# Two graph layers on one core: no memsets between groups of gathers, and a first layer with paired slot products and stationary type weights

## The chip, the cores and the metric

The kernel runs on one core of a Trainium2 chip. The metric is the device time of one execution in microseconds. Before the change the median of three runs is 4864.73 us (4861.53 to 4864.73).

## The reference, cut to what matters

There are 12,500 nodes with 64 features, and 212,500 edges sorted by destination, each with 8 attributes and one of 16 types. All is fp32.

```python
h = jnp.maximum(_layernorm(x, axis=-1), 0.0)
for r in range(16):                                    # first layer
    mask = etypes == r
    msg = msg + h[src] * mask[:, None] @ weight[r]     # weight: 16 x 64 x 64
x = x + segment_sum(msg, dst)
h = jnp.maximum(_layernorm(x, axis=-1), 0.0)
msg_input = concatenate([h[src], h[dst], edge_attr], axis=1)   # second layer
msg = relu(msg_input @ W1 + b1) @ W2 + b2
x = x + segment_sum(msg, dst)
```

## The kernel before, in words

Edges are handled in groups of 1024: 8 tiles (`T`) of 128 edges (`P`), 208 groups (`G`) in all. Loops run over 26 turns (`NIT`) of 8 groups (`U`); the first turn of each layer is written out, the others run in a hardware loop, the last one of POOL and PE again by itself. Each engine has its own program; semaphores order them.

**Gathers.** For each tile POOL issues one indirect DMA (`gather`, L710) that fetches 128 rows of 64 fp32 from a table in DRAM (`h_table` in the first layer, `p_table` in the second) into `rows[:, u, t]`, so 8 for a group. `rows` has 8 buffers, one for each `u`. At the end of each group in `turn_of_rows` and `turn_of_groups` POOL writes zeros into a tile that nobody reads, `spacer` (L743, L763), and before the next group it waits until that write is done (`spaced`). It then waits for `slots_summed`, so that group k is gathered only when group k-3 has been summed by PE (first layer), or for `pre_added`, so that it is gathered only when DVE has added the rows of group k-3 (second layer). The gathers of groups 8 to 15 stand before `turn_of_rows`: they have no spacer, and wait only until the group 8 places earlier is summed. `wait_apart` is a wait followed by an increment of a semaphore that nobody reads.

**First layer.** DVE makes `onehot` (L1095): for each edge a row of 256 zeros with a one at type*16 + offset of its destination within 16 nodes. In `sum_slots` (L1379) PE multiplies, for each tile, the rows (stationary, 128x64) by the onehot (moving, 128x256). Even tiles go to partitions 0 to 63 of the result, odd ones to 64 to 127, and odd and even groups have PSUM banks of their own (two each, `slot_ps`). ACT copies each half of a group into `slots` (L890). In `apply_types` (L1386), for each pair of groups, PE adds up 16 products, one for each type: `slots` of this type is stationary (128x128), the type's weights, twice on the diagonal of a 128x128 block, move. ACT copies the result to `nodes_t` (L894), and PE puts it into windows of 128 nodes with two products of 256 columns (`place_nodes`, L1393), with a matrix `place` that DVE makes from `key_p` (L1161). DVE adds the windows to `acc` (`add_windows`, L1158).

The order on PE within `step` is: `sum_slots` of group u; then, at even u, `apply_types` of the pair before, at odd u `place_nodes` of the pair before. At u = 4 and u = 7 of each turn PE also does the parts of a chunk of 480 nodes that are then complete (L1329, L1336, L1344, L1346). ACT's order is: both halves of group u, then at even u the copy for `place_nodes`.

**Second layer.** For each group PE does `products` (L1461, L1462), `place_z` (L1470), `sum_group` (L1466) and `pick_q` (L1456); DVE adds the gathered rows (L1219), masks and reduces (L1226, L1230), adds a window (L1239), and spreads q (L1243); ACT does the relu (L951).

Of the kernel before, what the change touches and what calls it, by code (L numbers as in the profile page):

```python
# [6 lines left out]
def gnn_kernel(nc, x, src, dst, edge_attr, edge_type, rel_weight, w1, b1, w2, b2, out):  # L7
# [39 lines left out]
    T2 = T // 2  # L47
    Q = 2 * T2
# [14 lines left out]
    NWL = 2 + 4 + T + 4  # L63
# [10 lines left out]
    with ctx:  # L74
# [26 lines left out]
        heads_i = sb("heads_i", [Q, NP, 2], i32)  # L101
        heads_f = sb("heads_f", [Q, NP, 2], fp32)
        key_p = sb("key_p", [P, NP, 2], fp32)
        place = sb("place", [P, 2, 2 * W1], fp32)
        nodes_t = sb("nodes_t", [P, 2 * D], fp32)
        spread = sb("spread", [Q, P], fp32)
        spread_first = sb("spread_first", [Q, P], fp32)
        slot_row_i = sb("slot_row_i", [1, P], i32)
        slot_row = sb("slot_row", [1, P], fp32)
        idx = sb("idx", [P, U, T], i32)  # L110
        spacer = sb("spacer", [P, T * D], fp32)
        rows = sb("rows", [P, U, T, D], fp32)
        onehot = sb("onehot", [P, 2, T, C0], fp32)
        slots = sb("slots", [P, 2, R, P], fp32)
# [27 lines left out]
        w_types = sb("w_types", [P, R, 2 * D], fp32)  # L142
# [55 lines left out]
        key_ps = ps[:, 7, 0:2 * NP]  # L198
# [58 lines left out]
        spaced = sem("spaced")  # L257
# [4 lines left out]
        heads_in = sem("heads_in")  # L262
        heads_float = sem("heads_float")
        key_turned = sem("key_turned")
        key_copied = sem("key_copied")
        typed = sem("typed")
        nodes_copied = sem("nodes_copied")
        place_made = sem("place_made")
        placed = sem("placed")
# [189 lines left out]
        def scattered_products(pe, n):  # L459
            def tile(t):  # L460
                pe.wait_ge(sc["dst_float", n], t + 1)
                pe.matmul(ps[:, 0, 0:P], s_dstf.broadcast_to([P, P]), ident[:], start=True, stop=True)
                if n == 0:
# [3 lines left out]
                    for half in range(2):  # L467
                        r = slice(half * R // 2, (half + 1) * R // 2)
                        last = pe.matmul(ps[:, 2 + half, :].rearrange("p (r m) -> p r m", m=D), s_gt[0:D, :], w_types[0:D, r, 0:D], start=True, stop=True)
# [68 lines left out]
        def _(sp):  # L538
# [23 lines left out]
            of_pairs = dst[0:(NP - 1) * 2 * GE].rearrange("(m q h e) -> q m h e", q=Q, h=2, e=P)[:, :, :, 0]  # L562
            for h in range(2):
                sp.dma_start(heads_i[:, 0:NP - 1, h], of_pairs[:, :, h], allow_slow_non_contiguous=True).then_inc(heads_in, 16)
            for b, first in ((0, (G - 2) * GE), (1, LAST)):
                sp.dma_start(heads_i[b * T2:(b + 1) * T2, NP - 1, :], dst[first:first + GE].rearrange("(q h e) -> q h e", h=2, e=P)[:, :, 0],
                             allow_slow_non_contiguous=True).then_inc(heads_in, 16)
# [112 lines left out]
        def _(pool):  # L680
            for v in (ident[:], again[:], spread[:], spread_first[:]):
                pool.memset(v, 0.0).then_inc(pool_chain, 1)
            pool.memset(blocks[:], 1.0).then_inc(pool_chain, 1)
            pool.wait_ge(pool_chain, 5)
# [6 lines left out]
            pool.wait_ge(pool_chain, 6)  # L691
# [7 lines left out]
            by_head = lambda v: v.rearrange("q (h w) -> q h w", w=W0)  # L699
            pool.affine_select(out=by_head(spread[:]), in_=by_head(spread[:]), compare_op=ALU.not_equal, fill=1.0, base=0,  # L700
                               pattern=[[-1, Q], [0, W0]], channel_multiplier=1).then_inc(consts_made, 1)
            by_first = lambda v: v.rearrange("q (h w) -> q h w", h=2)
            pool.affine_select(out=by_first(spread_first[:]), in_=by_first(spread_first[:]), compare_op=ALU.not_equal, fill=-1.0, base=0,
                               pattern=[[-T2, 2], [0, P // 2]], channel_multiplier=1).then_inc(consts_made, 1)
            pool.iota(by_first(slot_row_i[:]), pattern=[[P, 2], [1, P // 2]], base=0, channel_multiplier=0).then_inc(consts_made, 1)
            pool.wait_ge(consts_made, 10)
# [16 lines left out]
            with pool.If(fits > 0):  # L723
# [8 lines left out]
                pool.sem_inc(spaced, 1)  # L732

                def turn_of_rows(it, last=False):
                    for u in range(U):
                        wait_apart(pool, spaced, (it - 2) * U + u + 1)
# [6 lines left out]
                        pool.memset(spacer[:], 0.0).then_inc(spaced, 1)  # L743
# [8 lines left out]
            with pool.If(fits > 0):  # L752
                def turn_of_groups(it, last=False):
                    for u in range(U):
                        wait_apart(pool, spaced, (NIT - 2 + it) * U + u + 1)
# [7 lines left out]
                        pool.memset(spacer[:], 0.0).then_inc(spaced, 1)  # L763
# [11 lines left out]
        def _(act):  # L775
            act.sem_inc(relu_made, AHEAD)
            act.sem_inc(pq_copied, 1)

            act.wait_ge(blocks_cleared, 2)
            loads = [(w_types[h * D:(h + 1) * D, :, h * D:(h + 1) * D], rel_weight.rearrange("r k m -> k r m")) for h in range(2)]  # L780
# [99 lines left out]
            with act.If(fits > 0):  # L880
                def group(it, u):
# [16 lines left out]
                for u in range(U):  # L898
                    group(0, u)
                    if u % 2 == 0 and u >= 2:  # L900
                        copy_nodes(u // 2 - 1)
# [637 lines left out]
```

## Time and profile before

| what | value |
|---|---|
| median of three runs | 4864.73 us |
| profiled execution | 4855.4 us |
| its span, first to last instruction | 4853.2 us |
| POOL busy | 3380.0 us (70%) |
| PE busy | 2787.7 us (57%) |
| PE weight loads busy | 1549.3 us (32%) |
| DVE busy | 1468.1 us (30%) |
| ACT busy | 577.2 us (12%) |
| granted TensorE clock, mean | 0.692 of 2.4 GHz |

The profiled execution lies 9.3 us under the median of the runs, and 2.2 us of it are outside its span. The engines work side by side, so their busy times don't add up to the span. POOL's issuing of DMAs counts as busy (as DMA_INDIRECT); the transfers themselves do not.

### The profile page before, as it was taken

How to read it: one execution, taken by the hardware profiler on the slowest of the kernel's cores; microseconds unless marked ns; L12 is line 12 of the kernel's file. 1: busy time of each engine (PE TensorE's matmuls, PEld its weight loads, DVE VectorE, ACT ScalarE, POOL GpSimd, SP SyncE). 2: the span in 40 equal slices, each digit the busy share in tenths (PEclk: the TensorE clock that was granted, in tenths of full speed). 3: DMA queues.
4: the chain of work that ended last, by engine and by line, in shares of the span. 5: the costliest groups of instructions: out<-in, count | busy, mean ns of one | idle time of the engine just before them, and what ended most of it. 6: DMA issues, size and time to landing. Idle time of an engine off the chain costs nothing.

```text
span 4853.2 us, 37713 instructions
## 1 busy us (share of the span) xinstructions
PE 2787.7 (57%) x10310; PEld 1549.3 (32%) x10310; DVE 1468.1 (30%) x2002; ACT 577.2 (12%) x1139; POOL 3380.0 (70%) x3742
## 2 busy tenths in 40 slices
PE   2565665656556655656565565565555655656555
PEld 1343343434334433434332232222222222222222
DVE  6322222222222222222232333233332332332333
ACT  3111111111111111111110010010000000100000
POOL 7567667666666666676757767777777777777776
PEclk9777776677767777776766666666666666666666
DMA  4111111111111111111111112111111111211111
GB/s 102 20 27 25 25 27 25 25 27 25 25 25 27 25 26 26 25 25 27 25 29 31 29 31 31 29 31 31 29 31 29 32 31 29 32 31 32 29 31 28
DMA packets 391187, 144.15 MB, mean 30 GB/s; under 512 B 321650, under 2 KB 337323, under 8 KB 391163
## 3 DMA queue, kind: packets, MB, share of 16 engines
q0 software_dynamic: 106304, 109.07, 11.8%
q1 hardware_dynamic: 282245, 34.18, 4.9%
q10 hardware_dynamic: 2614, 0.62, 0.1%
q8 instruction: 10, 0.16, 0.0%
q14 instruction: 14, 0.11, 0.0%
HBM read 129.03 MB, written 12.83 MB: 29 GB/s over the span
## 4 chain that ended last, share of the span: by engine, by line
POOL 39%; issue 26%; another core or an unknown queue 17%; PE 12%; DVE 3%; ACT 1%; SPq 1%; DMA 1%; POOLq 0%; DVEq 0%; ACTq 0%
POOL rows L710 36%; PE ps L1379 4%; PE ps L1386 2%; POOL spacer L763 2%; PE ps L1462 1%; PE ps L1461 1%; PE ps L1393 1%; POOL spacer L743 1%; PE ps L1344 1%; PE ps L1346 1%; DVE z_slot L1230 0%; PE ps L1466 0%; DVE q_blk L1243 0%; DVE slots L1219 0%
## 5 line engine op out<-in xcount | busy, mean ns | idle before, releaser
L710 POOL DMA_INDIRECT rows<-p_table,idx x1661 | 1579.6, 951 | 702.0 <-issue 631.3
L710 POOL DMA_INDIRECT rows<-h_table,idx x1533 | 1452.1, 947 | 693.8 <-issue 506.6
L1461 PE MATMUL ps<-w_attr,attr_t 64*128 64x512 f32 x416 | 400.9, 1063 | 1004.8 <-DVE q_blk L1243 694.7
L1379 PE MATMUL ps<-onehot,rows 128*64 128x256 f32 x3328 | 661.8, 512 | 101.2 <-DMA rows<-h_table,idx 50.8
L1386 PE MATMUL ps<-w_types,slots 128*128 128x128 f32 x3328 | 518.2, 307 | 226.5 <-issue 201.6
L1095 DVE TENSOR_TENSOR onehot<-key,ps 128x2048 f32<-128x2048 f32 x209 | 474.6, 2279 | 439.5 <-remote 389.5
L1386 PEld LDWEIGHTS ps<-w_types,slots 128*128 128x128 f32 x3328 | 462.3, 215 | 314.1 <-issue 282.5
L1219 DVE TENSOR_TENSOR slots<-ps,rows 128x512 f32<-128x512 f32 x208 | 143.9, 692 | 1378.1 <-DMA rows<-p_table,idx 831.5
L1379 PEld LDWEIGHTS ps<-onehot,rows 128*64 128x64 f32 x3328 | 333.6, 179 | 349.4 <-issue 287.8
L1461 PEld LDWEIGHTS ps<-w_attr,attr_t 64*128 64x128 f32 x416 | 96.8, 288 | 1041.8 <-issue 1041.4
L1462 PE MATMUL ps<-q_blk,onehot 128*128 128x512 f32 x416 | 422.2, 1118 | 0.0
L890 ACT COPY slots<-ps 128x512 f32<-128x512 f32 x416 | 239.3, 588 | 1057.9 <-remote 766.6
L1466 PE MATMUL ps<-relus,onehot 128*128 128x512 f32 x416 | 339.8, 913 | 0.9 <-DVE z_blk L1226 0.9
L1158 DVE TENSOR_TENSOR acc<-acc,ps 64x128 f32 x208 | 58.2, 280 | 918.1 <-remote 645.7
L951 ACT ACTIVATE relus<-slots 128x512 f32<-128x512 f32 x208 | 131.1, 630 | 1663.2 <-DVE slots L1219 1511.3
L1393 PE MATMUL ps<-place,nodes_t 128*64 128x256 f32 x416 | 158.6, 521 | 277.8 <-ACT nodes_t L894 142.1
L1230 DVE TENSOR_REDUCE z_slot<-z_blk 128x64 f32<-128x512 f32 x208 | 209.1, 1005 | 0.1
L1226 DVE TENSOR_TENSOR z_blk<-ps,blocks 128x512 f32<-128x512 f32 x208 | 142.8, 687 | 193.5 <-remote 136.7
L1462 PEld LDWEIGHTS ps<-q_blk,onehot 128*128 128x128 f32 x416 | 100.8, 301 | 295.6 <-issue 295.6
L1393 PEld LDWEIGHTS ps<-place,nodes_t 128*64 128x64 f32 x416 | 70.4, 184 | 354.2 <-issue 185.7
L1470 PEld LDWEIGHTS ps<-onehot,z_slot 128*65 128x65 f32 x416 | 95.5, 230 | 231.5 <-issue 229.0
L1456 PEld LDWEIGHTS ps<-q_win,onehot 128*128 128x128 f32 x416 | 110.8, 267 | 176.4 <-issue 176.4
(142 smaller groups left out, 1971.8 us busy)
## 6 DMA issues: line engine op xcount, KB each, us to landing
rows<-p_table,idx POOLq DMA_INDIRECT x1661
rows<-h_table,idx POOLq DMA_INDIRECT x1533
attr<-in_edge_attr_dram SPq DMA_DIRECT2D x52, 128.0 KB
q_win<-q_table SPq DMA_DIRECT2D x208, 32.0 KB
p_table<-pq_out SPq DMA_DIRECT2D x25, 120.0 KB
q_table<-pq_out SPq DMA_DIRECT2D x25, 120.0 KB
out_dram<-xs SPq DMA_DIRECT2D x25, 120.0 KB
xs<-in_x_dram SPq DMA_DIRECT2D x6, 480.0 KB, 6.4
```

Source lines behind the costliest of these rows:

```text
L710: pool.indirect_dma_start(rows[:, u, t, :], None, table, bass.IndirectOffsetOnAxis(ap=at, axis=0)).then_inc(s, 16)
L890: act.copy(to, slot_ps[:, u % 2, t, :].rearrange("p t (r w) -> p t r w", w=W0)).then_inc(slots_copied, 1)
L1095: dve.tensor_tensor(onehot[:, b], key0[:, bass.ds(g, 1), :].rearrange("p a (t c) -> p (a t) c", c=1).broadcast_to([P, T, C0]), iota_ps.rea ...
L1219: dve.tensor_tensor(presum[:, u % 2, 0:T * D], pre_ps[:, u % 2, :], rows[:, u].rearrange("p t d -> p (t d)"), ALU.add).then_inc(pre_added, 1)
L1226: dve.tensor_tensor(by_tile(z_blk[:]), by_tile(z_ps), own_tile, ALU.mult).then_inc(z_masked, 1)
L1230: dve.tensor_reduce(z_slot[:, u, 0:D], z_blk[:].rearrange("p (t d) -> p d t", d=D), X, ALU.add).then_inc(z_slotted, 1)
L1379: last = pe.matmul(slot_ps[t % 2 * D:(t % 2 + 1) * D, b, t // 2, :], rows[:, u, t, :], onehot[:, b, t, :], start=True, stop=True)
L1386: last = pe.matmul(nodes_ps, slots[:, b, r, :], w_types[:, r, :], start=(r == 0), stop=(r == R - 1))
L1393: last = pe.matmul(win_ps, nodes_t[:, h * D:(h + 1) * D], place[:, h, :], start=(h == 0), stop=(h == 1))
L1461: pe.matmul(pre_ps[:, u % 2, :], attr_t[half, u // 2, :], w_attr[half].rearrange("k j d -> k (j d)"), start=True, stop=False)
L1462: pe.matmul(pre_ps[:, u % 2, :], oh1_t[:, u, :], q_blk[:, u % 2, :], start=False, stop=True).then_inc(pre_made, 1)
L1466: pe.matmul(z_ps, oh1[:, u, :], relu_rows[:, u % 2, :], start=True, stop=True).then_inc(z_made, 1)
```

## The change

The memsets of `spacer` and the waits for them go, in both layers. In the first layer:

- `sum_slots` multiplies two tiles at a time: the rows of both are stationary (128x128), the onehots of both move (128x512). The result holds four blocks, of which two are wanted (tile 2j's rows with its own onehot, and 2j+1's with its own). There are 4 products a group, each fills a bank, and all groups use the same 4 banks. So PE waits, before the first half of a group, until ACT has copied the first half of the group before, and likewise with the second half.
- ACT takes the wanted blocks out, with 4 copies of 64 partitions and 256 elements for each half in place of one of 128 partitions and 512.
- `apply_types` has the weights of two types as the stationary operand (128x64) and moves `slots` of the pair of groups (256 columns), 8 products a pair. Its result is 64x256, features by slots, so it must be turned: ACT copies it (`copy_sums`), PE turns it (`turn_nodes`, two transposes, ahead of `sum_slots` at odd u), ACT copies it again (`copy_nodes`, now ahead of the group at odd u), and `place_nodes` places it, with two products of 128 columns.
- `place` is made from `key_w`, which was there already, with half the columns. The loads, products and copies that made `key_p` go, and the clearing of `w_types`.

```diff
-        slot_ps = ps_all[:, 0:4 * 512].rearrange("p (b t c) -> p b t c", b=2, t=T2)
-        nodes_ps = ps[:, 4, 0:2 * D]
+        slot_ps = ps_all[:, 0:4 * 512].rearrange("p (j c) -> p j c", j=TH)
+        sums_ps = ps[0:D, 4, 0:2 * P]
+        nodes_ps = ps[:, 4, 2 * P:2 * P + 2 * D].rearrange("p (b m) -> p b m", m=D)
...
 def turn_of_rows(it, last=False):
     for u in range(U):
-        wait_apart(pool, spaced, (it - 2) * U + u + 1)
         if u % B == 0:
             wait_apart(pool, batch_in[u // B], 16 * (it - 1))
         wait_apart(pool, slots_summed, 2 * AHEAD + 2 * (it * U + u - 2))
         for t in range(SKIP if last and u == U - 1 else 0, T):
             gather(h_table, u, t, rows_in[u])
-        pool.memset(spacer[:], 0.0).then_inc(spaced, 1)
...
 def turn_of_groups(it, last=False):
-        wait_apart(pool, spaced, (NIT - 2 + it) * U + u + 1)
...
         for j in range(SKIP if last and u == U - 1 else 0, T):
             gather(p_table, u, j, rows_in[u])
-        pool.memset(spacer[:], 0.0).then_inc(spaced, 1)
...
     for half in range(2):
         act.wait_ge(slots_summed, 2 * AHEAD + 2 * g + half + 1)
-        t = slice(half * T2 // 2, (half + 1) * T2 // 2)
-        to = slots[:, u // 2 % 2].rearrange("p r (b t w) -> p b t r w", b=2, t=T2)[:, u % 2, t]
-        act.copy(to, slot_ps[:, u % 2, t, :].rearrange("p t (r w) -> p t r w", w=W0)).then_inc(slots_copied, 1)
+        j = slice(half * TH // 2, (half + 1) * TH // 2)
+        to = slots[:, u // 2 % 2].rearrange("p r (b j a w) -> p b a j r w", b=2, a=2, w=W0)[:, u % 2]
+        for a in range(2):
+            of = slot_ps[a * D:(a + 1) * D, j, a * C0:(a + 1) * C0].rearrange("p j (r h w) -> p h j r w", h=2, w=W0)
+            for h in range(2):
+                last = act.copy(to[h * D:(h + 1) * D, a, j], of[:, h])
+        last.then_inc(slots_copied, 1)
+
+def copy_sums(m):
+    act.wait_ge(typed, AHEAD + m + 1)
+    act.copy(sums_t[:], sums_ps).then_inc(sums_copied, 1)

 def copy_nodes(m):
-    act.wait_ge(typed, AHEAD + m + 1)
+    act.wait_ge(nodes_turned, m + 1)
     act.copy(nodes_t[:], nodes_ps).then_inc(nodes_copied, 1)
...
     for u in range(U):
+        if u % 2 == 1:
+            copy_nodes(it * (U // 2) + u // 2 - 1)
         group(it, u)
         if u % 2 == 0:
-            copy_nodes(it * (U // 2) + u // 2 - 1)
+            copy_sums(it * (U // 2) + u // 2 - 1)
...
 def sum_slots(g, it, u, first):
-    if u % 2 == 0 and (not first or u >= 2):
-        wait_apart(pe, slots_copied, 2 * (g - 1))
+    wait_apart(pe, slots_copied, 2 * g + 1)
     pe.wait_ge(onehot0, g + 1)
     pe.wait_ge(rows_in[u], ...)
-    for t in range(T):
-        last = pe.matmul(slot_ps[t % 2 * D:(t % 2 + 1) * D, b, t // 2, :], rows[:, u, t, :], onehot[:, b, t, :], start=True, stop=True)
-        if t % 4 == 3:
+    for j in range(TH):
+        if j == TH // 2:
+            wait_apart(pe, slots_copied, 2 * g + 2)
+        last = pe.matmul(slot_ps[:, j, :], rows[:, u, 2 * j:2 * j + 2, :].rearrange("p t d -> p (t d)"),
+                         onehot[:, b, 2 * j:2 * j + 2, :].rearrange("p t c -> p (t c)"), start=True, stop=True)
+        if j % 2 == 1:
             last.then_inc(slots_summed, 1)

 def apply_types(m, b):
-    pe.wait_ge(slots_copied, 4 * (m + 1))
-    for r in range(R):
-        last = pe.matmul(nodes_ps, slots[:, b, r, :], w_types[:, r, :], start=(r == 0), stop=(r == R - 1))
+    pe.wait_ge(slots_copied, 4 * m + 6)
+    for r in range(R2):
+        last = pe.matmul(sums_ps, w_pairs[:, r, :], slots[:, b, r, :], start=(r == 0), stop=(r == R2 - 1))
     last.then_inc(typed, 1)
+
+def turn_nodes(m):
+    wait_apart(pe, sums_copied, m + 1)
+    for b in range(2):
+        last = pe.transpose(nodes_ps[:, b, :], sums_t[:, b * P:(b + 1) * P], ident[0:D, 0:D])
+    last.then_inc(nodes_turned, 1)

 def place_nodes(m):
-    for h in range(2):
-        last = pe.matmul(win_ps, nodes_t[:, h * D:(h + 1) * D], place[:, h, :], start=(h == 0), stop=(h == 1))
+    for b in range(2):
+        last = pe.matmul(win_ps[:, b * W1:(b + 1) * W1], nodes_t[:, b, :], place[:, b, :], start=True, stop=True)

 def step(it, u, first=False):
+    if u % 2 == 1 and (not first or u >= 2):
+        turn_nodes(m - 1)
     sum_slots(k, it, u, first)
```

## Rows read from the trace of the kernel before

**Rows 1.** The page: span, and busy times with shares.

```profile
span 4853.2 us, 37713 instructions
PE 2787.7 (57%) x10310; PEld 1549.3 (32%) x10310; DVE 1468.1 (30%) x2002; ACT 577.2 (12%) x1139; POOL 3380.0 (70%) x3742
```

**Rows 2.** Groups by line: busy us, mean ns of one, idle time before and releasers.

```profile
L710 POOL DMA_INDIRECT rows<-p_table,idx x1661 | 1579.6, 951 | 702.0 <-issue 631.3 <-POOL spacer L763 63.5 <-DVE slots L1219 7.3
L710 POOL DMA_INDIRECT rows<-h_table,idx x1533 | 1452.1, 947 | 693.8 <-issue 506.6 <-remote 101.7 <-POOL spacer L743 59.3
```

**Rows 3.** Timeline of POOL across a spacer: start, length, what, idle before.

```profile
226.47 0.95 POOL L710 DMA_INDIRECT rows<-h_table,idx  x1 [0.96 <-issue]
...
235.23 0.95 POOL L710 DMA_INDIRECT rows<-h_table,idx  x1 [0.30 <-issue]
236.17 0.55 POOL L743 MEMSET spacer<- 128x512 f32 x1
237.69 0.95 POOL L710 DMA_INDIRECT rows<-h_table,idx  x1 [0.97 <-issue]
```

**Rows 4.** Gathers alone by stretch: length, busy us (count), granted clock, DMA share, GB/s.

```profile
1300.00:2300.00 1000.00, 650.54 (x687) 0.71 0.13 26
2500.00:3500.00 1000.00, 665.84 (x702) 0.66 0.19 30
```

**Rows 5.** Timeline of POOL where groups 8 to 15 are gathered without spacers.

```profile
138.41 0.95 POOL L710 DMA_INDIRECT rows<-h_table,src_tab  x1 [4.54 <-remote]
...
157.16 0.95 POOL L710 DMA_INDIRECT rows<-h_table,src_tab  x1 [0.30 <-issue]
161.39 0.95 POOL L710 DMA_INDIRECT rows<-h_table,src_tab  x1 [3.28 <-remote]
```

**Rows 6.** Timeline of PE and ACT in that stretch.

```profile
143.02 3.84 PE L1386 MATMUL ps<-w_types,slots 128*128 128x128 f32 x32
146.78 2.15 PE L1379 MATMUL ps<-onehot,rows 128*64 128x256 f32 x16
160.97 0.27 ACT L894 COPY nodes_t<-ps 128x128 f32<-128x128 f32 x1 [17.24 <-remote]
161.29 1.54 PE L1393 MATMUL ps<-place,nodes_t 128*64 128x256 f32 x3 [12.36 <-ACT nodes_t L894]
```

**Rows 7.** Waits, longest first: engine, line, releaser: us in total, times, longest.

```profile
ACT nodes_t L894 <- remote: 735.2, 79, 27.6
```

**Rows 8.** Timeline of PE while POOL stood still.

```profile
202.65 1.95 PE L1379 MATMUL ps<-onehot,rows 128*64 128x256 f32 x16
204.43 0.81 PE L1393 MATMUL ps<-place,nodes_t 128*64 128x256 f32 x3
...
207.11 3.84 PE L1386 MATMUL ps<-w_types,slots 128*128 128x128 f32 x32
```

**Rows 9.** By stretch: length, busy us (count) of PE, PEld, DVE, ACT, POOL, granted clock.

```profile
194.00:214.00 20.00, 18.84 (x154) 14.46 (x150) 12.14 (x13) 6.20 (x13) 0.02 (x1) 1.00 0.02 3
```

**Rows 10.** Timeline of PE at the lower clock, in the first layer and in the second.

```profile
1542.55 3.68 PE L1379 MATMUL ps<-onehot,rows 128*64 128x256 f32 x16
1546.16 3.66 PE L1386 MATMUL ps<-w_types,slots 128*128 128x128 f32 x19
...
3023.03 2.07 PE L1462 MATMUL ps<-q_blk,onehot 128*128 128x512 f32 x2
```

**Rows 11.** Groups by line: ACT's copies and a chunk's products, first layer.

```profile
L890 ACT COPY slots<-ps 128x512 f32<-128x512 f32 x416 | 239.3, 588 | 1057.9 <-remote 766.6 <-PE ps L1379 240.6 <-issue 50.6
...
L1344 PE MATMUL ps<-w1ab,h_t 128*120 128x256 f32 (+1 forms) x104 | 61.3, 695 | 173.8 <-issue 90.5 <-ACT h_t L860 83.3
...
L860 ACT COPY h_t<-ps 128x240 f32<-128x240 f32 (+1 forms) x26 | 9.5, 365 | 43.4 <-remote 37.3 <-issue 4.4 <-PE ps L1336 1.7
```

**Rows 12.** Second layer: DVE's addition of the gathered rows (by line), PE's products (in time).

```profile
L1219 DVE TENSOR_TENSOR slots<-ps,rows 128x512 f32<-128x512 f32 x208 | 143.9, 692 | 1378.1 <-DMA rows<-p_table,idx 831.5 <-remote 275.2 <-PE ps L1462 170.7
...
3031.84 2.04 PE L1461 MATMUL ps<-w_attr,attr_t 64*128 64x512 f32 x2 [4.68 <-DVE q_blk L1243]
```

More of the change, by code:

```diff
@@ L62, in gnn_kernel @@
     EG = 6
-    NWL = 2 + 4 + T + 4
+    NWL = 3 + 4 + T + 4
     GB = G + B
@@ L100, in gnn_kernel @@
         base_row = sb("base_row", [1, G], i32)
[L101 to L109, printed above, removed]
+        place = sb("place", [P, 2, W1], fp32)
+        sums_t = sb("sums_t", [D, 2 * P], fp32)
+        nodes_t = sb("nodes_t", [P, 2, D], fp32)
         idx = sb("idx", [P, U, T], i32)
-        spacer = sb("spacer", [P, T * D], fp32)
         rows = sb("rows", [P, U, T, D], fp32)
         onehot = sb("onehot", [P, 2, T, C0], fp32)
-        slots = sb("slots", [P, 2, R, P], fp32)
+        slots = sb("slots", [P, 2, R2, 2 * P], fp32)
         relus = sb("relus", [P, 2, T, KA], fp32)
@@ L141, in gnn_kernel @@
         zrows = sb("zrows", [P, D], fp32)
-        w_types = sb("w_types", [P, R, 2 * D], fp32)
+        w_types = sb("w_types", [D, R, D], fp32)
+        w_pairs = sb("w_pairs", [P, R2, D], fp32)
         w_attr = sb("w_attr", [2 * T * F, T, D], fp32)
@@ L468, in tile @@
                         r = slice(half * R // 2, (half + 1) * R // 2)
-                        last = pe.matmul(ps[:, 2 + half, :].rearrange("p (r m) -> p r m", m=D), s_gt[0:D, :], w_types[0:D, r, 0:D], start=True, stop=True)
+                        last = pe.matmul(ps[:, 2 + half, :].rearrange("p (r m) -> p r m", m=D), s_gt[0:D, :], w_types[:, r, :], start=True, stop=True)
                 else:
@@ L698, in _ @@
             pool.iota(limit_i[:], pattern=[[HG, 2]], base=-DONE, channel_multiplier=1).then_inc(consts_made, 1)
[L699 to L706, printed above, removed]
+            pool.wait_ge(consts_made, 7)
             def gather(table, u, t, s, of=None):
@@ L776, in _ @@
             act.sem_inc(relu_made, AHEAD)
+            act.sem_inc(slots_copied, 2)
             act.sem_inc(pq_copied, 1)
-            act.wait_ge(blocks_cleared, 2)
-            loads = [(w_types[h * D:(h + 1) * D, :, h * D:(h + 1) * D], rel_weight.rearrange("r k m -> k r m")) for h in range(2)]
+            act.wait_ge(blocks_cleared, 1)
+            loads = [(w_pairs[h * D:(h + 1) * D, :, :], rel_weight.rearrange("(r h) k m -> h k r m", h=2)[h]) for h in range(2)]
+            loads += [(w_types[:], rel_weight.rearrange("r k m -> k r m"))]
             loads += [(w1ab[half * D:(half + 1) * D, half, a * D:(a + 1) * D], w1[a * D:(a + 1) * D, :])
@@ L920, in _ @@
                 turn_of_groups(NIT - 1, last=True)
+                copy_sums(NP - 1)
+                copy_ht(NC - 1, chunk_nodes)
                 copy_nodes(NP - 1)
-                copy_ht(NC - 1, chunk_nodes)
                 act.wait_ge(layer0_summed, 1)
@@ L1004, in _ @@
             dve.tensor_copy(idx[:, 0:EG, :].rearrange("p u t -> p (u t)"), ps[:, 5, 0:EG * T]).then_inc(first_idx, 1)
-            dve.memset(w_types[:], 0.0).then_inc(blocks_cleared, 1)
             def check_edges():
@@ L1160, in make_place @@
                 def make_place(m):
-                    dve.tensor_tensor(place[:], key_p[:, bass.ds(m, 1), :].rearrange("p a (h c) -> p (a h) c", c=1).broadcast_to([P, 2, 2 * W1]),
-                                      iota_ps.rearrange("p (a c) -> p a c", a=1).broadcast_to([P, 2, 2 * W1]), ALU.is_equal).then_inc(place_made, 1)
+                    dve.tensor_tensor(place[:], key_w[:, bass.ds(2 * m, 2)].rearrange("p (b c) -> p b c", c=1).broadcast_to([P, 2, W1]),
+                                      iota_ps[:, 0:W1].rearrange("p (a c) -> p a c", a=1).broadcast_to([P, 2, W1]), ALU.is_equal).then_inc(place_made, 1)
                 def step(it, u, first=False):
@@ L1421, in _ @@
                 turn_h(NC - 1, chunk_nodes)
+                turn_nodes(NP - 1)
                 place_nodes(NP - 1)
```

43 lines of the change are left out of this document (12 added, 31 removed).

## The prediction, made before the changed kernel was run

> **What bounds the kernel now.** I read the page first. POOL is the busiest engine, 3380.0 us of 4853.2, PE follows with 2787.7 [rows 1]. The groups by line say that POOL's time is gathers: 3322 of them, of which the 1661 of the second layer take 951 ns each and the 1533 of the first layer's main part 947, and that the idle time ahead of them is mostly "issue", which waits for nothing [rows 2]. The timeline shows the beat. Gathers follow each other after 0.95 + 0.30 = 1.25 us. At a group's end stands a memset of 0.55 us, and 0.97 us pass before the next gather; from 226.47 to 237.69 is 11.22 us for a group [rows 3]. By stretch, the first layer makes 687 gathers in 1000 us, 8 x 1000/687 = 11.64 us a group, the second 702, so 11.40 us [rows 4]. So in both layers POOL runs near its own beat of 11.22; the other engines add 0.42 and 0.18 us a group. The page's 57% for PE is a mean over two layers with different work: what matters is whether PE and its partners keep up at a shorter beat.
>
> **The change, part by part.**
>
> *Spacers.* A group would then be 8 x 1.25 = 10.0 us, if its waits cost nothing on POOL. The 16 gathers from 138.41 are such a stretch: the last starts at 157.16, 18.75 us later, which is 15 x 1.25, with a group's boundary between them at no cost [rows 5]. So the beat falls by 1.22 us a group. 192 groups of the first layer (those after 8 to 15) and 208 of the second have a spacer: 400 x 1.22 = 488 us is the most that can be won. From below, nothing: what ends the wait may be the others.
>
> *Slot products, PE.* Before, 16 instructions (each fp32 product is recorded as two) of 256 columns take 1.95 us at the full clock, 2.4 GHz [rows 8, 9], and 3.68 us at 1.2 GHz [rows 10]. That is 0.12 us for each. After, 8 instructions of 512 columns with 128 weights. The row nearest to them is L1462, two of 512 columns in 2.07 us at the lower clock; L1393 had three of 256 columns in 0.81 us at the full one, an instruction each 0.21 to 0.27. So I take 0.43 us at the full and 0.9 at the lower clock for each: 3.4 and 7.2 us a group. This part adds 1.5 us to a group at one clock and 3.5 at the other. The reason is in these rows: before, instructions of 256 columns into different halves of the partitions advance by 0.12 us, those of L1393 into the same half by at least 0.21. The Trainium skill, "TensorE: Matmul & The Clock Gate", section "Part 3: Packing small matmuls — row/col tiling", says that products with few weight columns, put into different column groups of the array, run side by side. It speaks against this change, which gives that up and computes two unwanted blocks of four; by it alone the slot products would cost twice what they did, as the rows say too.
>
> *Types, PE.* Before, 32 instructions of 128 columns with 128 weights took 3.84 us [rows 8], at the lower clock 3.66 x 32/19 = 6.2. After, 16 of 256 columns with 64 weights: 3.4 at the full clock (0.21 each) and 6.8 at the lower. No gain to speak of in columns; half the weight loads.
>
> *Placing and turning, PE.* Two products of 128 columns for two of 256 save 0.4 to 0.85 us a pair, the two transposes cost 0.3 to 0.5: nothing.
>
> So a pair of groups costs PE 6.8 + 3.4 + 0.8 = 11 us at the full clock, 14.4 + 6.8 + 1.4 = 22.6 at the lower, where before it was 8.6 and 15. The parts for node chunks come on top: L1344 has 61.3 us in 104 pairs, 0.6 us [rows 11], the bias products next to it the like, the turns less, so I estimate 1.5 us a pair. The new beat of POOL is 20.0 us a pair. It fits at the full clock and doesn't at the lower one. The first layer had 0.71 on average [rows 4]; at 0.71 the pair takes 11 / 0.71 = 15.5 us, and 17.0 with the chunks, which fits with 3.0 us left.
>
> *ACT.* For each half 4 copies of 256 elements in place of one of 512 (588 ns); the nearest is L860 with 365 ns for 240 elements [rows 11]. 8 x 0.38 = 3.0 us a group for 1.2. A pair has 0.4 + 0.3 us of copies more (L894 takes 0.27 [rows 6]). 6.8 us of 20: hidden, but the copy of a half, 1.5 us, now stands between PE's groups, because the banks are shared. PE has the other half to do meanwhile, 1.7 us at least, so that wait is near zero as long as ACT hears of the end of a half at once.
>
> *Waits.* New is that PE waits at each odd u, ahead of the slot products, for ACT's `copy_sums`, which waits for the end of `apply_types`. Behind that wait stand the group's products, then ACT's copies, then POOL's gathers of three groups on. At least it costs 0.4 us of copy and some 0.1 of signals, a pair. At most it costs what ACT waits for that end today: 735.2 us in 79 times, 9.3 each [rows 7], since PE's instructions are recorded well before others may start on them. I take 2 us a pair, near the low end, because there are half the weight loads in the stretch behind which these delays stand, and because the second layer, with few and long products, shows little of them.
>
> *Before the loops* the clearing of `w_types` and the making of `key_p` go: a few us. I take 4.
>
> *The sum.* First layer: 17.0 + 2 = 19.0 us of PE a pair against 20.0 of POOL, so they catch each other at times. I take 11.0 us a group, 1.0 over the beat for 0.42 today: 192 x (11.64 - 11.0) = 123 us. Second layer: only the beat changes. DVE waits for the DMA of rows 831.5 us in 208 groups, 4.0 each, though only a part of this can be given up [rows 12]: PE's products (2.04 + 2.07) and DVE's addition stand in a ring with it. I take 10.5, 0.5 over the beat: 208 x (11.40 - 10.5) = 187 us. With the 4, 314 us: the profiled execution goes from 4855.4 to 4541, and the median of the runs from 4864.7 to **4551 us**. For both layers together: each 0.1 us a group is 40 us.
>
> **The rivals.**
>
> *POOL's beat alone decides.* The others add what they add today: 10.42 and 10.18 us a group, 4864.7 - 488 - 4 = 4373. For it: DVE and ACT are far from full [rows 1]. Against it: PE's 19.0 of 20.0. Chance 0.2 for all below 4460.
>
> *The gap was needed.* In the stretch without spacers PE's products of types end by the record at 146.86, yet ACT starts on them at 160.97, when POOL had come to rest after 157.16; POOL then goes on at 161.39, 22.98 us after 138.41, so 11.49 us a group, no shorter than with spacers [rows 5, 6]. When POOL issues without a pause, PE's results may be reported late until POOL must stop. For both layers: 192 x 0.15 less and 208 x 0.09 more, 4850 us. For it is that it is the one place where the trace shows what the change makes. Against: it has another set of waits (8 groups ahead), first passes through written-out code, and PE has the old products. Chance 0.2 for 4700 to 4875.
>
> *PE's ring becomes the bound in the first layer; slower.* It needs the pair's PE time with its waits to go over 23.3 us. Its work is 17.0, so the first layer gets slower when the waits take 6.3 us a pair. With the 9.3 that ACT waits today it is 26.3 us a pair, 13.15 a group: 192 x 1.51 = 290 us more. Against 187 + 4 won elsewhere that makes 4964 us, and 5151 if the second layer gains nothing. The kernel as a whole gets slower at 8.3 us of waits (191/192 = 0.99 a group over 11.64). Against it: a PE that works more is granted the higher clock more often (full in the 20 us when it was busy for 18.84 [rows 9]), and POOL at rest lets its results through. Chance 0.25 for all above 4875.
>
> **How the numbers follow.** The forecast, 4460 to 4700, has 0.35, the three rivals 0.2, 0.2 and 0.25. A difference of 0.2% (10 us) is about what a measurement of this kernel can tell. Faster by more: the forecast, the first rival, and 0.12 of the second: 0.66. Within: 0.04. Slower: 0.05 of the second and the third, 0.30. The range for 8 in 10 leaves out 0.04 below 4370 and 0.15 above 4990, and it is wide because the cases have both signs; the forecast's own is 4460 to 4700.
>
> **What would show it.** Right: POOL has no idle time but 0.30 between most gathers; 10.4 to 10.6 us a group in the second layer and some 11 in the first; slot products 8 instructions in 3.4 to 7 us; DVE's wait for DMA in the second layer shrinks by about 0.9 us a group; clock in the first layer above 0.71. Wrong: idle times of 3 us and more ahead of the first gather of each second group, ended by PE or DVE; `copy_sums` starting 5 us or more after the end of L1386; PE waiting at `turn_nodes`, with the clock still at 0.7.

## The result, and the profile after

The changed kernel takes 5270.03 us (median of four runs, 5226.03 to 5293.56) against 4864.39 for the kernel before: 1.0825 of it, 95% interval 1.0751 to 1.0899. It is slower by 406 us; the forecast of 4551 and its range are missed, on the wrong side.

The page of the changed kernel: its span, the busy times, and the granted clock in 40 slices.

```profile
span 5278.6 us, 32488 instructions
...
PE 2864.8 (54%) x7184; PEld 1316.7 (25%) x7184; DVE 1454.3 (28%) x1998; ACT 991.8 (19%) x2490; POOL 3152.3 (60%) x3337
...
PEclk9877787787877877877856666666666666666666
```

POOL is busy for 228 us less, most of it the memsets, and PE for only 77 us more than in [rows 1]; yet the span is 425 us longer. Only ACT is nearer to its limit than before (19% for 12%), and it is far from it. The groups by line of the same page:

```profile
L688 POOL DMA_INDIRECT rows<-p_table,idx x1661 | 1572.5, 947 | 1050.1 <-DVE slots L1199 527.9
L688 POOL DMA_INDIRECT rows<-h_table,idx x1533 | 1447.2, 944 | 985.6 <-issue 462.5
...
L1356 PE MATMUL ps<-onehot,rows 128*128 128x512 f32 x1664 | 972.2, 735 | 125.1 <-ACT slots L867 76.9
L867 ACT COPY slots<-ps 64x256 f32<-64x256 f32 x1664 | 608.9, 366 | 1061.0 <-remote 599.9
...
L1370 PE MATMUL ps<-ident,sums_t 64*128 64x64 f32 x208 | 39.7, 283 | 825.4 <-ACT sums_t L872 695.7
...
L1364 PE MATMUL ps<-slots,w_pairs 128*64 128x256 f32 x1664 | 390.6, 389 | 1.0 <-ACT slots L867 1.0
```

The gathers last as long as in [rows 2]. POOL's idle time ahead of them has grown by 640 us, and the memsets that are gone gave back 217 of it. Second layer: 1572.5 + 1050.1 = 2622.6 us, before 1579.6 + 702.0 = 2281.6 and 208 memsets of 0.55, 2396. That is 227 us more. First layer: 2432.8 against 2145.9 + 192 x 0.55 = 2251.5, 181 more. Together that is 408 of the 425. So more of the loss lies in the second layer, in which only the memsets and their waits changed. By stretch, as in [rows 4]:

```profile
1300.00:2300.00 1000.00, 606.01 (x643) 0.79 0.12 24
...
2700.00:4700.00 2000.00, 1215.89 (x1286) 0.64 0.17 28
```

8 x 1000/643 = 12.44 us for a group of the first layer (11.64 before), and 8 x 2000/1286 = 12.44 in the second too (11.41 before, 1402 gathers in the same stretch). The stretch of the second layer starts at 2700 here, because the first layer's gathers now go on until some 2610. The new waits of the trace (engine, line, releaser: us in total, times, longest):

```profile
PE ps L1448 <- DVE q_blk L1223: 1026.9, 125, 21.0
PE ps L1370 <- ACT sums_t L872: 695.7, 54, 18.9
ACT slots L867 <- remote: 599.9, 84, 16.3
POOL rows L688 <- DVE slots L1199: 527.9, 80, 11.4
POOL rows L688 <- PE ps L1356: 342.2, 32, 39.0
```

In the second layer PE now waits 1026.9 us for DVE (694.7 before), and POOL 527.9 us (7.3 in [rows 2]). What such a wait looks like in the first layer, from the timeline (start, length, what, idle time before):

```profile
1484.23 3.67 PE L1364 MATMUL ps<-slots,w_pairs 128*64 128x256 f32 x16
...
1500.22 0.94 POOL L688 DMA_INDIRECT rows<-h_table,idx  x1 [0.30 <-issue]
1505.26 0.36 ACT L872 COPY sums_t<-ps 64x256 f32<-64x256 f32 x1 [13.27 <-remote]
1505.77 0.45 PE L1370 MATMUL ps<-ident,sums_t 64*128 64x64 f32 x2 [17.88 <-ACT sums_t L872]
...
1513.68 0.94 POOL L688 DMA_INDIRECT rows<-h_table,idx  x1 [12.52 <-PE ps L1356]
```

The products by types end at 1487.90. ACT, which waits for nothing else, starts on them at 1505.26, 17.4 us later and 4.1 us after POOL's last gather ended. Then everything follows at once. It is the picture of [rows 5, 6], in the loop now, and POOL stands for 12.52 us in place of 3.28.

### The profile page after: what moved, and what is told of

Its sections match the earlier page's. It is cut to its first block, busy times and chain, and to the rows that moved or that the text cites. A ratio compares the mean times of both kernels' runs of the same rounds, so it can differ in the third digit from the quotient of the medians.

```text
span 5278.6 us, 32488 instructions
## 1 busy us (share of the span) xinstructions
PE 2864.8 (54%) x7184; PEld 1316.7 (25%) x7184; DVE 1454.3 (28%) x1998; ACT 991.8 (19%) x2490; POOL 3152.3 (60%) x3337
## 3 DMA queue, kind: packets, MB, share of 16 engines
q0 software_dynamic: 106304, 109.07, 10.8%
## 4 chain that ended last, share of the span: by engine, by line
another core or an unknown queue 34%; PE 32%; issue 19%; DVE 8%; ACT 5%; DVEq 1%; ACTq 0%; DMA 0%; SPq 0%
PE ps L1356 14%; PE ps L1449 5%; PE ps L1448 4%; ACT slots L867 4%; PE ps L1364 3%; PE ps L1453 3%; DVE z_slot L1210 2%; DVE q_blk L1223 2%; DVE slots L1199 1%; DVEq L1214 1%; PE ps L1457 1%; PE ps L1377 1%; PE ps L1370 1%; DVE onehot L1182 1%
## 5 line engine op out<-in xcount | busy, mean ns | idle before, releaser
L688 POOL DMA_INDIRECT rows<-p_table,idx x1661 | 1572.5, 947 | 1050.1 <-DVE slots L1199 527.9
L1448 PE MATMUL ps<-w_attr,attr_t 64*128 64x512 f32 x416 | 362.0, 966 | 1266.5 <-DVE q_blk L1223 1026.9
L1356 PE MATMUL ps<-onehot,rows 128*128 128x512 f32 x1664 | 972.2, 735 | 125.1 <-ACT slots L867 76.9
L867 ACT COPY slots<-ps 64x256 f32<-64x256 f32 x1664 | 608.9, 366 | 1061.0 <-remote 599.9
L1356 PEld LDWEIGHTS ps<-onehot,rows 128*128 128x128 f32 x1664 | 368.8, 235 | 583.0 <-issue 578.2
L1370 PE MATMUL ps<-ident,sums_t 64*128 64x64 f32 x208 | 39.7, 283 | 825.4 <-ACT sums_t L872 695.7
L1364 PE MATMUL ps<-slots,w_pairs 128*64 128x256 f32 x1664 | 390.6, 389 | 1.0 <-ACT slots L867 1.0
L1364 PEld LDWEIGHTS ps<-slots,w_pairs 128*64 128x64 f32 x1664 | 223.7, 140 | 212.7 <-issue 70.1
L1370 PEld LDWEIGHTS ps<-ident,sums_t 64*128 64x128 f32 x208 | 26.5, 177 | 858.7 <-issue 858.7
L1223 DVE TENSOR_TENSOR q_blk<-ps,blocks 128x512 f32<-128x512 f32 x208 | 142.1, 683 | 217.8 <-remote 193.3
L928 ACT COPY attr_t<-ps 128x128 f32<-128x128 f32 x105 | 27.8, 264 | 748.9 <-remote 624.6
```

The costliest lines, as they stand in the source:

```text
L688: pool.indirect_dma_start(rows[:, u, t, :], None, table, bass.IndirectOffsetOnAxis(ap=at, axis=0)).then_inc(s, 16)
L867: last = act.copy(to[h * D:(h + 1) * D, a, j], of[:, h])
L1223: dve.tensor_tensor(by_tile(q_blk[:, u % 2, :]), q_ps.rearrange("p (a d) -> p a d", a=1).broadcast_to([P, T, D]), own_tile, ALU.mult).then ...
L1356: last = pe.matmul(slot_ps[:, j, :], rows[:, u, 2 * j:2 * j + 2, :].rearrange("p t d -> p (t d)"), onehot[:, b, 2 * j:2 * j + 2, :].rearra ...
L1364: last = pe.matmul(sums_ps, w_pairs[:, r, :], slots[:, b, r, :], start=(r == 0), stop=(r == R2 - 1))
L1448: pe.matmul(pre_ps[:, u % 2, :], attr_t[half, u // 2, :], w_attr[half].rearrange("k j d -> k (j d)"), start=True, stop=False)
```

## The experiments

"Late" below means that ACT or DVE starts on something of PE well after PE's record of it ends. The 15 kernels were measured in eight sessions, each on another chip, and the chip turned out to matter more than the kernel. On four chips the kernel before took 4743 to 4753 us, on three 4858 to 4867, as in the first measurement, and on one 4940. I call the first four ordinary and the others late. Within a session the times of the kernel before agree within 0.6%. Ratios are always to its times in the same session.

"remote" in a wait is the trace's word for a semaphore update that it can put down to no engine's work that ended just before. It tells the two kinds of chip apart without exception: the nine traces from ordinary chips have not one such wait, the eight from late chips (the two of the first measurement among them) have 374 to 731 each.

| kernel | ordinary chips | late chips |
|---|---|---|
| before | 4743 to 4753 us | 4858 to 4867 (one: 4940) |
| before, memset of one column | 4593.81 (0.9665), 4589.52 (0.9658) | 4942.69 (1.0173) |
| before, memset without the wait | 4408.64 (0.9275) | 5065.22 (1.0264, where before takes 4940) |
| before, no memsets | 4216.18, 4206.66, 4215.48 (0.887) | 5160.77 (1.0632) |
| changed, memsets put back | 4756.07 (1.0007) | 4879.77 (1.0036) |
| changed | 4211.58 (0.8878) | 5270.03 (1.0825), 5232.20 (1.0572, where before takes 4940) |

**The two halves of the change, each alone.** The kernel before without memsets:

```diff
-        wait_apart(pool, spaced, (it - 2) * U + u + 1)
...
-        pool.memset(spacer[:], 0.0).then_inc(spaced, 1)
...
-        wait_apart(pool, spaced, (NIT - 2 + it) * U + u + 1)
...
-        pool.memset(spacer[:], 0.0).then_inc(spaced, 1)
```

> The kernel before, with only the memsets and the waits for them taken out in both layers. Theory A (the gap between groups lets PE's results be reported; without it they come late until POOL has to stop): slower than before in both layers, 12 to 13 us a group, 5000 to 5400 us. Theory B (the gap costs only time, and the changed first layer's ring of PE and ACT made the change slow): POOL's shorter beat is won, some 10.5 us a group in both layers, 4450 to 4600 us.

And the changed kernel with those four lines put back (with the tile and the semaphore that they use):

> The changed kernel with memsets and waits put back in both layers. Theory A: the second layer is back at 11.4 us a group as before, the first near it, 11.5 to 12; 4850 to 4950 us. Theory B: the second layer no faster than in the changed kernel, the first still at 12.4 us a group or above; 5050 us or more.

Measured, on one chip where the kernel before takes 4752.93 us: 4216.18 without memsets (0.8871, 0.8856 to 0.8886) and 4756.07 with the first layer changed alone (1.0007, 0.9997 to 1.0016). Gathers by stretch of the kernel without memsets:

```profile
1300.00:2300.00 1000.00, 737.52 (x780) 0.75 0.17 31
2500.00:3500.00 1000.00, 756.08 (x801) 0.67 0.22 35
```

The second layer runs at 9.99 us a group, POOL's own beat. The first does too, by 801 gathers over 1000 to 2000 us; the 780 of the stretch shown are fewer because the change of layers, at some 2100 us, lies in it. Both times are below what either theory expected. This was as much against the first measurement as a result can be: the half that can save time saves 537 us, the other half nothing, and no loss appears.

**The pause made smaller.** Two steps between a full memset and none. First, two buffers for the zeros, and a wait only for the memset of the group before last, so that POOL writes them but does not stand still:

```diff
-        spacer = sb("spacer", [P, T * D], fp32)
+        spacer = sb("spacer", [P, 2, T * D], fp32)
...
-        pool.sem_inc(spaced, 1)
+        pool.sem_inc(spaced, 2)
...
-        pool.memset(spacer[:], 0.0).then_inc(spaced, 1)
+        pool.memset(spacer[:, u % 2], 0.0).then_inc(spaced, 1)
```

> The kernel before, with the memsets kept, but each group waits for the memset of the group before last, so that POOL's sequencer may run ahead. Theory A1 (a pause in the gathers is what counts): the pause shrinks to the memset's 0.55 us; the time depends on whether this is enough, 4700 to 5200 us. Theory A2 (what counts is that the sequencer is held until POOL's engine is empty): as slow as with no memset at all, above 5000 us.

Second, the wait kept and one column cleared:

```diff
-        pool.memset(spacer[:], 0.0).then_inc(spaced, 1)
+        pool.memset(spacer[:, 0:1], 0.0).then_inc(spaced, 1)
```

> The kernel before, with memsets of one column in place of 512, and the wait for them kept. Theory A1 (pause): the pause falls from 1.5 to some 1.0 us; if the time falls by 400 x 0.45 = 180 us to 4690, the pause is longer than is needed; if it rises, the length of the pause counts. Theory A2 (the held sequencer): 4650 to 4720 us.

Measured: 4408.64 us (0.9275, 0.9257 to 0.9294) and 4593.81 (0.9665, 0.9645 to 0.9684). By gathers over 1000 to 2000 us, the groups take 10.42 (768 gathers) and 10.91 us (733). So of the 1.31 us between 11.31 (707 gathers in the kernel before, on an ordinary chip) and 10.0, the memset itself costs some 0.4 and standing still for its end 0.9. On these chips a pause is pure cost, for its length. Both times are again below all that was expected (4650 us and more).

**The changed kernel again, beside before and the memset half.** Three kernels unchanged, to see whether the contradiction lay in the kernels or in the chip.

> The changed kernel once more, because the kernel before took 4753 us in the last call and 4864 us beside the changed kernel. Theory C (the chip or core of the first measurement let PE's results be seen late while POOL gathers without a pause; another chip doesn't): where the kernel before takes 4753 us, the changed one takes 4200 to 4500 us; where it takes 4864 us, 5270 us as before. Theory D (the paired products and the missing gap together make it slow on any chip): 5150 to 5300 us in either case.

> The kernel before, for its trace on the chip of this call. Theory C: where it takes 4753 us, ACT starts on the products of types within 0.1 us of their end by the record (waits named by PE, none as unknown), and the first layer has 11.2 us a group. Theory D: the waits of the first trace, 9 us each and of unknown origin, are there again.

> The kernel before without memsets once more. Theory C: 4216 us where the kernel before takes 4753 us; where it takes 4864 us, above 5000 us. Theory D: 4216 us in either case.

Measured: the changed kernel 4211.58 us (0.8878, 0.8863 to 0.8893), before 4743.03, and without memsets 4206.66 (0.8869, 0.8851 to 0.8886). The same changed kernel was 5270.03 in the first measurement. So the contradiction did not lie in the kernels, as theory C has it. Here it gets POOL's beat, 802 gathers in the stretch 2500 to 3500. Waits of the changed kernel on this chip:

```profile
DVE slots L1199 <- DMA rows<-p_table,idx: 1336.7, 206, 7.2
...
ACT slots L867 <- PE ps L1356: 920.0, 414, 8.7
```

DVE's addition waits for nothing but the rows, ACT's copies of `slots` for nothing but the products that they need, and no wait is "remote". Those of the kernel before on it, where [rows 7] had 735.2 us in 79 times of "remote":

```profile
DVE slots L1219 <- DMA rows<-p_table,idx: 1624.5, 207, 8.7
ACT slots L890 <- PE ps L1379: 1469.7, 412, 11.2
ACT nodes_t L894 <- PE ps L1386: 372.2, 104, 4.3
```

In the timeline above, "remote" was a product that had ended long ago. On an ordinary chip each of the 104 copies is released by the end of PE's product; on a late one 79 are not. By the stretches of [rows 4] the kernel before takes 11.30 us a group in the first layer on this chip (708 gathers) and 11.36 in the second (704). So of the 0.42 us over POOL's beat of 11.22 that the prediction put down to the work of the other engines in the first layer, 0.34 were lateness; of the 0.18 in the second, only 0.04.

**Lateness made by hand.** Before without memsets, and in the second layer DVE hears of PE's products only by way of ACT, after five copies of 1024 zeros, some 5.4 us:

```diff
+    act.wait_ge(pre_made, AHEAD + it * U + u + 1)
+    for again in range(5):
+        act.wait_ge(unread_done, (it * U + u) * 5 + again + 1)
+        last = act.copy(unread[:], zero[:].broadcast_to([P, 1024]))
+        last.then_inc(unread_done, 1)
+    act.wait_ge(unread_done, (it * U + u + 1) * 5 + 1)
+    act.sem_inc(pre_late, 1)
...
-    dve.wait_ge(pre_made, AHEAD + it * U + u + 1)
+    dve.wait_ge(pre_late, it * U + u + 1)
```

> The kernel before without memsets; in the second layer DVE learns of the end of PE's products by way of ACT, which makes 5 copies of 1024 zeros to a tile that nobody reads in between, some 5.5 us. It asks how late a result may be. In the trace without memsets the ring of the second layer (DVE's addition to q_blk, PE's products, back to the addition) takes 7.2 us of POOL's 10.0. Theory C (late results make the chip of the first measurement slow): 7.2 + 5.5 + signals = 12.8 us a group in the second layer, near the 12.4 to 12.6 of the first chip; 208 x 2.8 = 580 us more than 4207 to 4216, so some 4790 us. Rival: POOL's distance of three groups hides lateness, and the second layer stays at 10.0 us a group, 4210 us. On a chip where the kernel before takes 4864 us: above 5200 us.

It met a chip on which before takes 4866.75 us: 5250.05 us, 1.0785 (1.074 to 1.0829). So it could not show what 5.4 us of lateness do to a kernel that has none. It showed something else: its first layer, untouched and without memsets, makes 659 gathers in 1000 to 2000 us, 12.14 us a group, where the same code on the two chips before made 801 and 802. The second makes 1259 in 2700 to 4700, 12.71 us a group. The kernel without memsets was then measured a third time. It met an ordinary chip (before 4752.44) and took 4215.48, 0.8875 (0.8849 to 0.8901).

> The kernel before without memsets a third time, to meet the chip on which the kernel before takes 4865 us (it did in the last call). Theory C: there, above 5000 us, slower than with memsets, in both layers; on a chip where the kernel before takes 4743 to 4753 us, 4207 to 4216 us. Rival C2 (on that chip only the paired products' ring suffers, and the second layer only because of something else in the changed kernel): 4300 to 4700 us there.

**Both halves alone, on a late chip.** The first two experiments once more, on a chip where before takes 4864.40 us (4864.39 in the first measurement).

> The kernel before without the memsets and their waits. If the kernel before takes about 4865 us on this chip (the condition in which PE's results are seen late while POOL gathers without a pause), the theory that the gap was needed there expects 12.1 to 12.7 us per group in both layers as in the run with late DVE, so 5150 to 5350 us, slower than before by 6 to 10%; the rival, that only the changed first layer or the late DVE brought the loss, expects under 4600. If the kernel before takes about 4750 us, all theories expect 4205 to 4220 us, and the run tells only that this chip is of the other kind.

> The changed kernel with the memsets and their waits put back. Where the kernel before takes about 4865 us: the theory that the gap was needed expects the time back near that of before, 4780 to 4950 us; the rival, that the changed first layer with its longer chain through PE and ACT loses by itself, expects above 5050. Where the kernel before takes about 4750 us, 4750 to 4760 us from both.

Measured: without memsets 5160.77 us (1.0632, 1.0594 to 1.0669); changed, with memsets, 4879.77 (1.0036, 1.0024 to 1.0049). Gathers by stretch without memsets:

```profile
1300.00:2300.00 1000.00, 619.96 (x657) 0.70 0.13 25
...
2700.00:4700.00 2000.00, 1249.73 (x1316) 0.64 0.18 29
```

12.18 and 12.16 us a group. With the memsets back, the changed kernel has 687 and 702 in the stretches of [rows 4], exactly as there. This settles the question of the halves: on a late chip, taking the pause away loses 6.3%, with PE's and ACT's programs as they were. The changed first layer alone loses 0.36%.

The trace shows what differs. The kernel without memsets on this chip, in time; POOL gathers every 1.25 us through the whole stretch, until 1535:

```profile
1528.84 0.37 PE L1382 MATMUL ps<-w_types,slots 128*128 128x128 f32 x1 [1.03 <-issue]
...
1530.27 0.37 PE L1382 MATMUL ps<-w_types,slots 128*128 128x128 f32 x1 [1.06 <-issue]
...
1534.09 0.94 POOL L710 DMA_INDIRECT rows<-h_table,idx  x1 [0.30 <-issue]
1534.47 0.37 PE L1382 MATMUL ps<-w_types,slots 128*128 128x128 f32 x1 [0.33 <-issue]
...
1536.57 2.62 PE L1382 MATMUL ps<-w_types,slots 128*128 128x128 f32 x8 [1.73 <-issue]
```

The same kernel on an ordinary chip, POOL gathering in the same way:

```profile
1507.24 4.72 PE L1382 MATMUL ps<-w_types,slots 128*128 128x128 f32 x32
...
1512.00 0.27 ACT L890 COPY nodes_t<-ps 128x128 f32<-128x128 f32 x1 [4.07 <-PE ps L1382]
```

Here 32 products take 4.72 us, and ACT starts 0.04 us after them. On the late chip the 32 that begin at 1523.12 end at 1539.19, 16.1 us. Between them PE waits for nothing that the trace knows; they need no other engine. The clock doesn't explain it: it was granted at 0.70 from 1522 to 1536 and at 0.79 in the ordinary stretch, and even at 0.50 the 32 would take twice the 3.84 us of [rows 8], an estimate of 7.7. From 1536.57 on, 1.5 us after POOL's last gather ended (1534.09 + 0.94), the products follow each other again: the last eight take 2.62 us. Waits of the kernel without memsets on the late chip:

```profile
PE ps L1457 <- DVE q_blk L1239: 887.2, 112, 20.7
PE ps L1382 <- issue: 314.2, 307, 8.4
...
ACT slots L886 <- remote: 774.1, 127, 21.1
ACT nodes_t L890 <- remote: 630.3, 46, 27.6
```

307 such gaps ahead of L1382; on the ordinary chip that line has none. So a late chip has two signs: PE starts its products late, and others learn late of those that are done. That both have one cause is likely, but not shown.

**How much pause is needed.** The two smaller pauses on late chips. The memset of one column first met an ordinary one (before 4749.75): 4589.52 us, 0.9658 (0.9642 to 0.9675).

> The kernel before with a memset of one column, its wait kept. Where the kernel before takes about 4865 us: if any stop of POOL in each group is enough to free PE's results, the beat is the 10.90 us per group of the run on the ordinary chip or a little more and the time 4600 to 4750 us, a version that beats before there too; if the stop must be as long as before's, results come late again and the time is above 4900 us. Where the kernel before takes about 4750 us: 4590 to 4600 us from both.

> The kernel before with a memset of one column, its wait kept, once more. Where the kernel before takes about 4865 us: if any stop of POOL in each group is enough to free PE's results, the beat is about 10.90 us per group or a little more and the time 4600 to 4750 us; if the stop must be as long as before's, results come late again and the time is above 4900 us. Where the kernel before takes about 4750 us: 4585 to 4600 us from both.

> The kernel before with two spacer buffers, each memset waiting only for the one two groups before. Where the kernel before takes about 4865 us: if POOL must stand still, results come late as without memsets, 4950 to 5200 us, above the 1.017 of the memset of one column; if the stretch of 0.55 us of memset is what frees them, 4500 to 4850 us. Where it takes about 4750 us: 4400 to 4415 us from both.

> The changed kernel again. Where the kernel before takes about 4865 us: 5200 to 5300 us, a ratio near the first measurement's 1.0825, of which 1.063 is the memsets' as the kernel without them showed. Where it takes about 4750 us: 4205 to 4220 us.

Measured on late chips: one column with its wait 4942.69 us, 1.0173 (1.0156 to 1.0190), before 4857.55. A full memset without the wait 5065.22, 1.0264 (1.0221 to 1.0306), and in the same session the changed kernel 5232.20, 1.0572 (1.0526 to 1.0617), before 4939.71. The expectation that any stop is enough (4600 to 4750) is refuted, and so is that the write of zeros helps without a stop (4500 to 4850). Against an ordinary chip the late one costs, by the table: 4865/4750, 2.4%, with the full pause (4.0% on the chip of 4940), 4943/4592, 7.6%, with the short one, 5065/4409, 14.9%, without the wait (on the chip of 4940), and 5161/4213, 22.5%, with no pause. The ratios within a session give the same order: 1.0173/0.966 = 1.053, 1.0264/0.9275 = 1.107 and 1.0632/0.887 = 1.199. The less POOL stands still, the more a late chip costs, step by step.

## Why the prediction was wrong

**The step that failed** is in the sum: "Second layer: only the beat changes", 10.5 us a group, and with it 11.0 for the first. It holds where nothing is late, and there it was too cautious: 9.99. On the chip of the measurement it is 12.44 in both. The mechanism was named among the rivals, "The gap was needed", at a chance of 0.2, and mis-sized: it took 11.49 us a group from the one stretch without memsets [rows 5, 6] as if it were the whole effect, and gave 4850. The measured excess over that, 12.44 - 11.49 = 0.95 in 400 groups, is 380 us: 4850 + 380 = 5230, and 40 us of the measured 5270 lie outside the two stretches. The argument against it, other waits and first passes through written-out code, was worth nothing: the loop is worse than that stretch. What the rows did say was that POOL's two consecutive groups were followed by a copy 14.1 us late, and that [rows 7] had the same in the loop. One reading was wrong as well: that the second layer "shows little" of these delays. [rows 12] has 275.2 us of "remote" ahead of DVE's addition, more than for PE (170.7), and on an ordinary chip there is none.

**The spacers.** At most 488 us, beat 10.0. The beat is right on an ordinary chip, and 537 us are won there, since before stands at 11.30 and 11.36 and not at 11.22. The first rival, POOL's beat alone, is what happens there; it kept 0.42 and 0.18 us a group for the others' work, of which 0.34 and 0.04 were lateness and the rest went with the memsets, so its 4373 us stand against a measured 4211.58 (before started from 4743 there).

**PE's and ACT's work.** Slot products were to take 3.4 us at the full clock and 7.2 at the lower; the timeline has 3.70, and 6.63 where the granted clock was 0.55. Types: 3.4 forecast, 3.67 measured at the full clock. ACT's copies: 0.38 forecast, 0.366 measured. One figure was read wrong, without effect on the sum: the 19 products of types in [rows 10] ran at a granted clock of 0.66 and not 0.50, so 6.2 us for 32 is no figure of the lower clock; by the 3.84 at the full clock it would be some 7.7, an estimate. The Trainium skill, "TensorE: Matmul & The Clock Gate", section "Part 3: Packing small matmuls — row/col tiling", has products in different column groups of the array run at the same time. The traces agree with it: 16 products into alternating halves in 1.95 us [rows 8], and 8 of twice the columns into all of the array, with two unwanted blocks beside the two wanted, in 3.70. All this lies beside POOL's 20 us a pair: with memsets 4756.07 against 4752.93, without them 4211.58 against 4206.66. The granted clock of the first layer's stretch rose to 0.79 from 0.71, as forecast.

**Waits.** The turn's wait for ACT was put at 2 us a pair, bounds 0.5 to 9.3. It is 695.7/104 = 6.7 on the late chip, and 42.9 us in 79 times, 0.4 a pair, on an ordinary one. So the third rival, PE's ring in the first layer, had the first of its conditions met (6.3 us of waits a pair for that layer to get slower), and its range, above 4875, holds the time. That the time fell into this range was luck, for it is not the cause: without that wait the kernel takes 5160.77 us all the same, and with it and the pause the loss is only 0.36%. The changed kernel is slower than the one without memsets by 109 us in the medians and by 155 in the two profiled executions, of which POOL's lines have 96 in the first layer and 60 in the second. The second has the same code in both, so chips or executions differ by that much too. What the changed first layer costs there on top of the missing pause is therefore not settled: 96 us by these rows, less if the 60 are chance. The signs named for a wrong prediction came: idle times of 3 us and more ahead of a gather (12.52), a copy over 5 us late (17.4), PE waiting at the turn. Only the clock was not still at 0.7 but at 0.79. Among the chances, 0.35 + 0.2 + 0.12 is 0.67 and not 0.66; the 0.2 of the second rival leaves 0.11 for that part.

**What stays open** is why PE is held up on some chips when POOL gathers without a stop. It is tied to the session and thus to the chip, or to what goes on around it; these two were not told apart. For the kernel without memsets, the instructions (36554), the packets of POOL's queue (106304) and those of the two instruction queues (10 and 13) are the same on both kinds, and so is the time that the packets of POOL's queue took: 11.2% of 5123.7 us on a late chip and 13.6% of 4212.3 on an ordinary one are some 573 us each, and another ordinary one has 614 (14.6% of 4203.1). So slower transfers are not what holds up PE.

What does differ is what the trace holds of the semaphores. The views of DMA issues end with the median time from issue to landing, which needs all 16 updates of each gather. The kernel without memsets on an ordinary chip has it, and on the late one it has none:

```profile
rows<-p_table,idx POOLq DMA_INDIRECT x1661, 2.4
...
rows<-p_table,idx POOLq DMA_INDIRECT x1661
```

The packed trace of this kernel has 66987 semaphore updates on the ordinary chip and 16461 on the late one. All traces from ordinary chips have 67 to 69 thousand, those from late chips 16 to 18 (32 with the lateness by hand). Whether updates came merged, or their records were lost, is not shown. And each time here comes with a clock and a span from the profiler, so no run shows the kernels without recording: that the recording itself takes part in holding up the engines on a late chip is a rival that was not tested.

The kernel before is the fastest of the versions tried on late chips, and the one without memsets (or the changed one) on ordinary ones. None beats both everywhere: the memset of one column wins 3.4% on one kind and loses 1.7% on the other.

## What to carry to other kernels

A pause that looks like waste on the busiest engine may be what keeps the others on time: before taking it out, look in the trace for results used late ("remote" waits, products that begin late for "issue"), compute what the loop would be if every group were like the worst stretch that has no pause, and give that case more than a small chance. When several waits of one trace are for no visible work, a beat plus "what the others add" is not a model of the kernel. And take the time of such a change on several chips: here the same two kernels compare as 0.888 and as 1.083.

## What was unexpected of the hardware

- The same kernel took 4743 and 4940 us on two chips, at mean granted clocks that hardly differ (0.70 and 0.69), with the spread within each session below 0.6%. The changed kernel took 4211.58 and 5270.03, 25% apart.
- On a late chip 32 products that wait for no other engine took 16.1 us in place of 4.72, seven of them 0.7 to 2.1 us apart, while POOL issued its gathers at an unchanged 1.25 us. A gather itself was not slower there: 944 and 950 ns on the late chip, 944 to 947 on ordinary ones, in the kernel without memsets.
- On a late chip a copy on ACT started 17.4 us after the record of the product that it needs ended, and 4.1 us after POOL had come to rest.
